# A three-layer GCN and a top-k feed-forward on one core: identity matmuls for the first layer's self loops, norm tiles spread out, spills reordered, a bank of its own for the product

## The reference, cut to what matters

```
x: (6250, 256) float32; src, dst: (200000,) int32 edges, many of them into low node numbers
x = x + gcn(layernorm(x))
x = x + ffn(layernorm(x))

gcn: edges + one self loop per node; deg = segment_sum(1, dst); norm = dinv[src] * dinv[dst]
  h = relu(conv(h, W1, b1)); h = relu(conv(h, W2, b2)); h = conv(h, W3, b3)
  conv(h, W, b) = segment_sum((h @ W)[src] * norm, dst) + b

ffn: weights = x @ wr + br; the 3124 rows of largest weight are chosen (top_k of half, less one)
  y = (gelu(x_sel @ w1 + b1) @ w2 + b2) * weight; out = x + y at the chosen rows
```

## Time and profile before

| what | value |
|---|---|
| median of 3 runs | 2052.75 us (2049.27 to 2053.6) |
| profiled execution | 2062.73 us, its span 2061.0 us |
| mean granted clock of PE | 0.959 of full |
| busy: PE, weight loads, DVE | 1861.0, 1068.9, 1054.3 us |
| busy: ACT, POOL | 528.7, 1161.9 us |
| table stores and fetches on SP | 34 + 66, 1568 KB each |

### The profile page before, as it was taken

The page is one execution under the profiler, slowest core; times in us unless marked ns, Lnnn a source line. Parts: engine busy times, 40 slices in busy tenths (PEclk is TensorE's granted clock), DMA queues, the critical chain, the costliest instruction groups (busy, mean ns, idle before and its releaser), DMA issues.

```text
span 2061.0 us, 28897 instructions
## 1 busy us (share of the span) xinstructions
PE 1861.0 (90%) x10168; PEld 1068.9 (52%) x10168; DVE 1054.3 (51%) x3267; ACT 528.7 (26%) x1126; POOL 1161.9 (56%) x1213
## 2 busy tenths in 40 slices
PE   6874789998899999988999999998899989999898
PEld 5762456665555556543445554544444434446665
DVE  7877688886566566631222221210345444786422
ACT  5824134333344455510211111110000000002120
POOL 5400674666676667523677777762477767762211
PEclk9965899999999999999999999999999999999999
DMA  7649143544455556574667766764588869854200
GB/s 255 195 168 306 40 153 122 178 152 153 158 196 184 178 196 208 193 266 146 212 224 242 239 229 224 233 238 154 205 301 306 308 214 332 312 183 145 63 24 24
DMA packets 170597, 405.02 MB, mean 197 GB/s; under 512 B 29436, under 2 KB 122546, under 8 KB 157657
## 3 DMA queue, kind: packets, MB, share of 16 engines
q1 hardware_dynamic: 119864, 265.05, 36.4%
q0 software_dynamic: 50592, 138.13, 21.2%
HBM read 284.18 MB, written 118.89 MB: 196 GB/s over the span
## 4 chain that ended last, share of the span: by engine, by line
PE 67%; POOL 10%; issue 9%; DVE 7%; DMA 5%; ACT 2%; POOLq 0%; DVEq 0%; ACTq 0%
PE ag L1246 21%; PE pw L1246 16%; PE ag L1258 9%; POOL space_rows L1835 6%; PE pw L1214 5%; PE both L1272 4%; PE pw L1340 3%; PE ag L1353 2%; PE pw L1353 2%; PE ag L1340 1%; PE both L1264 1%; POOL space_rows L1802 1%; POOL space_rows L1827 1%; DMA space_rows<-row_dram,src_s 1%; DMA extra<-space_tables 1%
## 5 line engine op out<-in xcount | busy, mean ns | idle before, releaser
L1835 POOL DMA_INDIRECT space_rows<-row_dram,src_s x947 | 967.9, 1022 | 378.7 <-issue 207.7
L1246 PE MATMUL ag<-space_a,space_ring 128*128 128x512 f16 x2107 | 628.9, 382 | 30.5 <-POOL space_ring L1843 30.5
L1214 PE MATMUL pw<-space_tables 128*128 128x147 f16 (+1 forms) x2022 | 330.1, 248 | 51.5 <-DVE space_tables L871 43.0
L1258 PE MATMUL ag<-space_rows,hots 128*128 128x512 f16 x947 | 359.6, 380 | 5.1 <-DMA space_rows<-row_dram,src_s 3.3
L1214 PEld LDWEIGHTS pw<-space_tables 128*128 128x128 f16 x2022 | 218.9, 116 | 238.5 <-DVE space_tables L871 68.8
L871 DVE TENSOR_TENSOR space_tables<-iota_two,space_tables 128x294 f16<-128x294 f16 (+1 forms) x1011 | 306.6, 338 | 0.0
L1582 ACT ACTIVATE space_ring<-pw 128x784 f16<-128x784 f32 (+1 forms) x257 | 220.1, 857 | 312.3 <-PE pw L1214 308.5
L1246 PEld LDWEIGHTS ag<-space_a,space_ring 128*128 128x128 f16 x2107 | 198.9, 98 | 133.5 <-issue 27.3
L868 DVE TENSOR_TENSOR space_tables<-iota_many,space_tables 128x512 f16<-128x512 f16 x506 | 215.2, 425 | 59.1 <-PE pw L1214 56.5
L1246 PE MATMUL pw<-space_b,space_ring 128*128 128x512 f16 x784 | 204.4, 381 | 6.4 <-DVE space_work L895 6.4
L1246 PE MATMUL pw<-space_a,space_ring 128*128 128x512 f16 x686 | 172.0, 381 | 1.9 <-DVE space_b L895 1.9
(11 more groups left out here) (407 smaller groups left out, 1926.8 us busy)
## 6 DMA issues: line engine op xcount, KB each, us to landing
space_ring<-adj SPq DMA_DIRECT2D x49, 1568.0 KB, 7.5
adj<-space_ring SPq DMA_DIRECT2D x34, 1568.0 KB, 6.2
space_tables<-adj SPq DMA_DIRECT2D x17, 1568.0 KB
extra<-hots SPq DMA_DIRECT2D x3, 6272.0 KB, 23.2
space_work<-extra SPq DMA_DIRECT2D x147, 128.0 KB
space_rows<-row_dram,src_s POOLq DMA_INDIRECT x947, 3.7
space_b<-in_x_turned SPq DMA_DIRECT2D x7, 896.0 KB, 13.6
space_a<-in_x SPq DMA_DIRECT2D x7, 896.0 KB, 5.4
```

The lines of the kernel that those rows point to most:

```text
L1214: pe.matmul(pw[v % 2][:, half, at_c:at_c + n], olo[:, j % RING // 2, :, j % 2 * 2 + i], ohi[:, j % RING, 0:n, i], start=s == FIRST[w], sto ...
L1246: mm = pe.matmul(bank(q), a[:, k, :], hh[l][:, k, :], start=i == 0 and not own, stop=i == TILES - 1)
L1258: pe.matmul(bank(q), hots_area[:, hot_at, :, g - SPOT_GROUPS[SPOT_GROUP_OF[g]][0]], slots[g % GR], start=False, stop=i == n).then_inc(g_us ...
L1835: pool.indirect_dma_start(slots[g % GR], None, row_dram[STEP_LAYER[g]], bass.IndirectOffsetOnAxis(src_s[:, s:s + 1], 0)).then_inc(g_in[g % ...
```

## The change

It has four parts. (1) In layer 1 the product ph goes into a PSUM bank of its own (half of pw[1]), and turn_tile waits for the ACT activation of the previous tile (relued) instead of its low half on DVE (lo_s). (2) The norm of layer 2 goes tile by tile: statistics with each sum, the root per group, then one normed tile each six units; the last group of four is split into 3 and 1; the choice starts earlier, and the first block's turns come ahead of begin_choice(1). (3) In the spill POOL starts before the layer's rows are stored and waits for that later, fetches the old rows early and overlaps the source rows with the hot; the eight row fetches ahead of it are gone; spills stand 20 units earlier, the sums of tiles 49 and 98 thirty units earlier (2159 to 2129, 4074 to 4044). (4) The self loops of tiles 0 to 30 in layer 0 are added by an identity matmul on PE (30 more of L1245); such a tile begins when ACT's copies are counted. POOL adds the loop to the table after the tile was aggregated (agg_d), at END instead of START in its order, and SP stores it 8 units later. The order of adds becomes ... 28 (unit 1733), 31 (1796), 29 (1800), 32 (1848), 30 (1858), 33 (1871). The first 16 row fetches stand before the add of table 0. Of the first fetches of layer 1, the third goes from unit 1871 to 1856, the fourth to 1879.

```diff
-NORMS = (7, 7, 7, 7, 5, 5, 7, 4)
+NORMS = (7, 7, 7, 7, 5, 5, 7, 3, 1)
...
-SPILL_AT = [END[0], START[TILES] + 170, START[2 * TILES] + 170]
-OVER_AT = [SPILL_AT[0] + 45, SPILL_AT[1] + 60, SPILL_AT[2] + 60]
+SPILL_AT = [END[0], START[TILES] + 150, START[2 * TILES] + 150]
+OVER_AT = [SPILL_AT[0] + 45, SPILL_AT[1] + 50, SPILL_AT[2] + 50]
...
+PE_LOOPS = DENSE[0] - 1
+LOOPS_AT = [END[DENSE_Q[n]] if n < PE_LOOPS else DUE[TILE_PAIR[n + 1] - 1] for n in range(TD)]
+LOOP_ORDER = sorted(range(TD), key=LOOPS_AT.__getitem__)
 FETCHED = [(l, n) for l in (1, 2) for n in range(DENSE[l])]
-FETCH_AT = [DUE[-1] if m == 0 or m < 4 and TD - 4 + m >= DENSE[0] else END[DENSE_Q[TD - 4 + m]] if m < 4 else END[DENSE_Q[DENSE[0] + m - 4]]
+FETCH_AT = [DUE[-1] if m == 0 else LOOPS_AT[TD - 4 + m] + 8 if m < 4 and TD - 4 + m >= DENSE[0] else END[DENSE_Q[TD - 4 + m]] if m < 4 else END[DENSE_Q[DENSE[0] + m - 4]]
             for m in range(len(FETCHED))]
-PE_LOOPS = 1
...
+NORM_TILE = [(g, i) for g, n in enumerate(NORMS) for i in range(n)]
+NORM_TILE_AT = [NORM_AT[g] + NORM_SPACE * (i + 1) if g < len(NORMS) - 1 else NORM_AT[g] for g, i in NORM_TILE]
+NORM_TILES_OF = by_unit(NORM_TILE_AT)
+ROOTED_OF = by_unit([u + 4 if g < len(NORMS) - 1 else u for g, u in enumerate(NORM_AT)])
 PAIR_OUT_AT = [u + 70 for u in NORM_AT]
...
-CHOICE_BEGINS, CHOICE_SPACE = 17.0, 4.0
+CHOICE_BEGINS, CHOICE_SPACE = 14.0, 3.8
...
-LOOPS_AT = [START[DENSE_Q[n]] if n < DENSE[0] else DUE[TILE_PAIR[n + 1] - 1] for n in range(TD)]
-STORES = by_unit([END[PE_LOOPS] + 4 if n == PE_LOOPS else DUE[TILE_PAIR[n + 1] - 1] for n in range(TD)])
+STORES = by_unit([u + 8 for u in LOOPS_AT])
...
-    px, ph = both[:, 0:D], both[:, D:2 * D]
+    px = both[:, 0:D]
+    ph = [both[:, D:2 * D], pw[1][:, 1, 0:D]]
...
-            def norm_group(g):
+            def spread_of_tile(k):
+                (g, i), t = NORM_TILE[k], Q[2 * TILES + k]
+                chained(dve.bn_stats(stats[:, i, :], nodes[:, t]))
+                chained(dve.bn_aggr(aggr[:, g % 2, i, :], stats[:, i, :]))
+            def spread_of_group(g):
                 n = NORMS[g]
...
+                chained(dve.tensor_scalar(rstd_x[:, g % 2, 0:n], aggr[:, g % 2, 0:n, 1], EPS, None, ALU.add))
+                steps[f"spread {g}"] = done_x["n"]
...
+            def rooted_group(g):
+                n = NORMS[g]
+                dve.wait_ge(root_s, g + 1)
+                chained(dve.reciprocal(rstd_x[:, g % 2, 0:n], rstd_x[:, g % 2, 0:n]))
+            def norm_tile(k):
+                (g, i), t = NORM_TILE[k], Q[2 * TILES + k]
+                if i == 0 and 0 < g <= EARLY_GROUPS:
+                    dve.wait_ge(pairs_out, 48 * NORM_FROM[g])
+                elif i == 0 and g and not XN_FROM[g]:
+                    dve.wait_ge(pairs_late, 48 * (NORM_FROM[g] - EARLY))
+                to = xn[:, XN_FROM[g] + i]
+                chained(dve.tensor_scalar(to, nodes[:, t], aggr[:, g % 2, i, 0:1], rstd_x[:, g % 2, i:i + 1], ALU.subtract, ALU.mult))
+                dve.tensor_tensor(nodes[:, t], nodes[:, t], to, ALU.add).then_inc(norm_s, 1)
+                dve.scalar_tensor_tensor(x_junk, to, 1.0, wr_b, ALU.mult, ALU.mult, accum_out=route[:, t:t + 1]).then_inc(stat_s, 1)
+                done_x["n"] += 1
...
+                            spread_of_tile(q - 2 * TILES)
                     for g in NORMS_OF.get(u, ()):
-                        norm_group(g)
-                        if g == EARLY_GROUPS - 1:
+                        spread_of_group(g)
+                    for g in ROOTED_OF.get(u, ()):
+                        rooted_group(g)
+                    for k in NORM_TILES_OF.get(u, ()):
+                        norm_tile(k)
+                        if k == EARLY - 1:
                             begin_choice(0)
...
             upto(UNITS + 300)
+            hidden_turns(0)
             begin_choice(1)
-            for c in range(len(BLOCKS) + 1):
+            for c in range(1, len(BLOCKS) + 1):
...
-                        if l == 0 and t == PE_LOOPS:
+                        if l == 0 and t < PE_LOOPS:
                             pe.wait_ge(evac, PER_TILE * (t + 1))
                         elif l == 0:
-                            pe.wait_ge(looped, t + (t < PE_LOOPS))
+                            pe.wait_ge(looped, LOOP_ORDER.index(t) + 1)
...
-                    own = l == 0 and t == PE_LOOPS
+                    own = l == 0 and t < PE_LOOPS
...
                 pe.wait_ge(summed, q + 1)
-                pe.wait_ge(lo_s, q)
+                pe.wait_ge(lo_s, min(q, TILES))
+                if q > TILES:
+                    pe.wait_ge(relued, q)
...
-                        moved(pool.indirect_dma_start(pair_i, None, edges, bass.IndirectOffsetOnAxis(edge_i, 0)))
+                        pool.indirect_dma_start(pair_i, None, edges, bass.IndirectOffsetOnAxis(edge_i, 0)).then_inc(more_in, 16)
+                        each(pool.tensor_tensor(base_of, item[:, 1:2], part_f[:], ALU.add))
+                        each(pool.tensor_copy(target_i, base_of))
+                        if l < 0:
+                            pool.wait_ge(deg_clear, 16)
+                        else:
+                            pool.wait_ge((stored_0, stored_s, stored_s)[l], 32 if l else 16)
+                        pool.indirect_dma_start(more_old[:, 0:width], None, target,
+                                                bass.IndirectOffsetOnAxis(target_i, 0)).then_inc(old_in, 16)
+                        landed(more_in)
+                        if l >= 0:
+                            pool.wait_ge(rows_out[l], 16 * (TILES if l else GROUPS))
+                            pool.indirect_dma_start(more_rows, None, row_dram[l],
+                                                    bass.IndirectOffsetOnAxis(pair_i[:, 1:2], 0)).then_inc(more_rows_in, 16)
...
-                        each(pool.tensor_tensor(base_of, item[:, 1:2], part_f[:], ALU.add))
-                        each(pool.tensor_copy(target_i, base_of))
                         if l >= 0:
...
-                            moved(pool.indirect_dma_start(more_rows, None, row_dram[l],
-                                                          bass.IndirectOffsetOnAxis(pair_i[:, 1:2], 0)))
+                            landed(more_rows_in)
                         pool.sem_inc(more_ready, 1)
                         pool.wait_ge(more_out, pool.snap(n))
                         pool.sem_inc(passed, 1)
...
-                        if l < 0:
-                            pool.wait_ge(deg_clear, 16)
-                        moved(pool.indirect_dma_start(more_old[:, 0:width], None, target,
-                                                      bass.IndirectOffsetOnAxis(target_i, 0)))
+                        landed(old_in)
...
             def add_loops(n):
                 pool.wait_ge(evac, PER_TILE * (n + 1))
-                if n == PE_LOOPS:
+                if n < PE_LOOPS:
                     pool.wait_ge(agg_d, n + 1)
...
             pool.wait_ge(tab_out, 16)
             spill(-1)
-            add_loops(0)
-            pool.wait_ge(rows_out[0], 16 * GROUPS)
-            pool.wait_ge(stored_0, 16)
             spill(0)
-            add_loops(PE_LOOPS + 1)
-            add_loops(PE_LOOPS)
-            n_looped = PE_LOOPS + 2
+            n_looped = 0
             for g in range(LAYER_STEP[1]):
-                while n_looped < TD and LOOPS_AT[n_looped] <= (STEP_UNIT[g - GR] + 40 if g >= GR else LOOPS_AT[1]):
-                    add_loops(n_looped)
+                while n_looped < TD and g >= GR and LOOPS_AT[LOOP_ORDER[n_looped]] <= STEP_UNIT[g - GR]:
+                    add_loops(LOOP_ORDER[n_looped])
                     n_looped += 1
                 fetch_row(g)
             while n_looped < TD:
-                add_loops(n_looped)
+                add_loops(LOOP_ORDER[n_looped])
                 n_looped += 1
...
             for l in range(1, 3):
-                pool.wait_ge(rows_out[l], 16 * TILES)
-                for g in range(LAYER_STEP[l], LAYER_STEP[l] + AHEAD):
-                    fetch_row(g)
-                if l == 1:
-                    pool.wait_ge(stored_s, 32)
                 spill(l)
                 if l == 1:
                     pool.wait_ge(m_v, 1)
                     pool.partition_all_reduce(small[:, 19:20], small[:, 18:19], P, RED.max).then_inc(m_p, 1)
-                for g in range(LAYER_STEP[l] + AHEAD, LAYER_STEP[l + 1]):
+                for g in range(LAYER_STEP[l], LAYER_STEP[l + 1]):
                     fetch_row(g)
...
             def store_tile(n):
-                if n == PE_LOOPS:
-                    sp.wait_ge(looped_late, 1)
-                else:
-                    sp.wait_ge(looped, n + (n < PE_LOOPS))
+                sp.wait_ge(looped, LOOP_ORDER.index(n) + 1)
...
-                    sp.dma_start(pair_dram[t * P:t * P + P, 0:D], xn[:, i]).then_inc(stored, 16)
```

(27 more changed lines are left out.)

41 lines of the change are left out of this document (7 added, 34 removed).

## The result

The changed kernel takes 2072.22 us (median of 4 runs, 2069.69 to 2074.27) against 2053.18 before: a ratio of 1.0095, 95% interval 1.0078 to 1.0113. It is slower by 19 us, where 11 us less were forecast; 2072 lies outside the range given (2012 to 2068). The profiled execution took 2072.68 us, its span 2070.9.

A forecast was written before the change was run, and what follows sets the result against it. PE, busy for 90% of the span, was taken as the bound. Terms summing to −10.5 us took the profiled 2062.73 us to 2052.2, times 0.9952 gave 2042 us, 0.5% less; range 2012 to 2068, the forecast's own 2027 to 2058.

The forecast's parts named there:

- part 3: End of layer 0: tables 28 to 30 leave their slots late, so PE waits for copies; +23 us (12 to 28).
- part 4: Layer 1: turn waits go, −13.5 us; spill waits, −5; eight fetches no longer done ahead, 0 to +2.
- Part 1: Early layer 0: table 0's add comes behind spill and 16 fetches, delaying tile 3's copy; +16 us (15 to 16.5).
- Part 2: Middle of layer 0: waits for POOL go, thirty identity matmuls are added; −18 us (−24.6 to −17).
- term 2: Same as Part 2: middle of layer 0, waits for POOL go, identity matmuls are added; −18 us.
- rival C: Tables come back late in middle layer 0, slow landings included, costing 3 to 7 us per tile; 2062 to 2070, 17%.
- Rival B: Early layer 0: DVE's run doesn't hold POOL, so clean-up takes 0.3 us; −5 to −1; 2021 to 2025, 17%.
- Parts 5 to 7: Layer 2: start, spill waits go, −12.5 us; norm groups, DVE pieces shorten, −14.5; end, settle copies wait for norm, +16.
- Part 8: Feed-forward: the choice starts 3 ticks earlier and its longest wait shrinks; −2 us (−5 to 0).
- A: Three new waits, early and end of layer 0 and end of layer 2, are hidden; 1983 us, 10%.
- D: Layer 0 tile starts: PE only trades POOL's add for ACT's last copy; 0 to +6.5 us, 2060 to 2066, 11%.

The follow-up runs named there:

- second profile: The kernel before, unchanged, profiled once more: 2047.97 us.

## Why the prediction was wrong

**The steps that failed** are three: the size of part 3; part 4's "the rows lead PE by more than that, so 0"; and, behind the sum, "2052.2 × 0.9952", which brings it to the median. In the first profile, on which the sum was made, it misses 21 us, of which part 3 is 17 and the rest of layer 1 is 10 (parts 1 and 2 came out 5 us better each). The other 9 us are the last step. The first profile took 10 us more than the median. By the second one (14.8 us less, and 15.9 less between tiles 3 and 39) its excess lies in the waits for POOL there, and term 2 takes just these waits out. The sum of 2052.2 us was thus a time of the changed kernel, whose own stage takes 455.2 to 455.3 us in eight profiles, with no such excess left in it; 0.9952 took the excess off a second time. Without it the forecast would have been 2052 us, no change. The forecast's own range, given as 2027 to 2058, is 2023 to 2061 by plain addition of its parts' ranges; the measured time lies outside either.

**Part 2** itself is 22.7 us in the first profile, 6.8 in the second, and about 12 in a median execution (467 less 455.3, an estimate), where 18 were forecast. A second profile has 17.3 us of the waits in place of 30.5. The cost side was right: the twofold identity matmul measures 0.22 us each where 0.216 was used.

**Part 3** had the mechanism (tables at the end leave late, two landings in series behind SP's fetch) and mis-sized it: +31 forecast for the stretch, +47.9 measured. I gave tile 31 one us and tile 30 nothing; PE stood 5.1 and 4.3 us for them, as the stores that free their slots (of tables 28 and 27) left at 835 and 810 us, each at the end of a tile, and landed 7 us later. For tile 32 it stood 12.2 us where +9 was in the sum: store(29) left at 864.4, 1.6 us behind store(31), and took 9.0 to land. For tile 33 it stood 15.7 where about 15 was forecast. That makes 37 us of stalls for 25; the other 11 us of the stretch are mostly the slow clock around four stalls, for which 5 was in the sum (an estimate, as what is left over). Putting tiles 27 to 31 back takes 47 us off, so the cause is shown. Store landings were 5.1 to 9.0 us, no slower than before; rival C's slow landings were not needed, and its place (mid layer 0) did not show.

**Part 1** had the right mechanism and was 6 too high. Five profiles of this early code sum tile 3 at 325.1 to 331.2 us where before has 320.1, so it is 5 to 11 too high by them. The stall was 35.5 us, and PE went on at 292.0 where 295 was forecast; a POOL operation was held by DVE's run (24.75 us, until PE, and so DVE, ran dry), and the 16 fetches cost 20 us. With the add of table 0 ahead of them it is 9.9 us, with 8.8 us behind it, and with tile 0 looped as before it is gone. Rival B, that POOL isn't held, is refuted by 24.75, 30.11 and 19.19 us. The Trainium skill's rule (SBUF — State Buffer, the section on who interferes with whom), by which the other engine waits for one instruction, doesn't describe these rows, where it waited for a whole run of DVE instructions. Not every hold lasted to the end of a run: the issue at 204.63 us was let go after 6.26 us, while DVE went on. That it is these ports which hold it was argued, not tried.

**Part 4.** The turn waits went, 13.5 us, as forecast, and the start of the layer was right (−18 against −18.0 and −19.2). What failed is "the rows lead PE by more than that, so 0": over the rest of the layer 11 us of row waits came. Not for the lost lead of eight fetches, as I then thought (putting them back leaves 16.4 us), but for the bank itself: alone it brings 11.7 us of them. POOL issues a fetch every 1.25 us without a pause through layer 1, 314 in 394 us, and the turn waits had lain under that. PE's saved time becomes waiting for rows; when the fetches take 13 us less, the row waits go.

**Parts 5 to 7** held in their mechanism: −13.0 for −12.5; −9.9 for −14.5, just outside its range; +17.5 for +16 at the end of layer 2, a stall of 16.7 us where 14 was forecast, by the mechanism named, and 15.6 us of it go when that norm is moved. Part 8 gave −2.8 and −5.1 where −2 was forecast.

**The rivals.** A and B fell. C would have ended near the measured time, but by another place. D fell in its reason: the waits moved to ACT's copies, as it said, though only where a store was late, and the middle gained as long as the tables came back.

What stays open: which resource holds POOL while DVE runs, and why some holds end before DVE's run does.

## What to carry to other kernels

When a producer's result also has to leave its buffer (here a table to be stored before its ring slot is written again), moving a small step behind the consumer costs nothing at the step and a whole round of queue and landing at the slot; look for the stretch where the schedule is tightest, above all its ends. A wait of one profiled execution is a sample: profile the kernel before more than once. And when that execution is slower than the median, ask in which waits it is slower: if the change removes them, its sum is already the new time and must not be scaled down to the median again. Before PE is freed of a wait, look which engine runs without a pause in that stage: if there is one, the wait only changes its name.

## What the runs showed of the hardware

A small GpSimd operation was held for 14 to 25 us, and the issue of one indirect DMA for up to 30.11 us, while DVE ran two-input float16 operations without a gap; they were let go within 1 us of DVE's stop. Shorter holds of an issue (6.26 us in the changed kernel) ended while DVE went on. An indirect DMA of 64 rows cost GpSimd 0.909 us and one of 128 rows 0.952: almost all of the price doesn't depend on the rows. The same kernel's profiles differ by 16 us in one stage (478.0 and 462.1 us) with nothing in it changed, while the eight profiles with single identity matmuls took 455.2 to 455.3 us in it.
